# Scores of the second and third attention: one head to each half of TensorE's rows, two banks at a time, keys kept in one copy

## What is computed

```python
# second attention
q, k, v = (x @ qkv_w + qkv_b)          # 12 heads of 64
q = layernorm(q, q_norm_w, q_norm_b); k = layernorm(k, k_norm_w, k_norm_b)
attn = softmax(einsum('bhqd,bhkd->bhqk', q * 64 ** -0.5, k))
o = einsum('bhqk,bhkd->bhqd', attn, v) * gates
# third attention
q, k, v = x @ w_qkv.T                  # 12 heads of 64
q = q * rsqrt(norm(q, over heads) + eps); k = k * rsqrt(norm(k, over heads) + eps)
scores = softmax(einsum('bhid,bhjd->bhij', q, k) / scale)
out = einsum('bhij,bhjd->bhid', scores, v) @ w_out.T + b_out
```

## Time and profile before

| | us |
|---|---|
| median of 3 runs | 1297.73 |
| lowest and highest run | 1296.96, 1299.48 |
| the profiled execution | 1300.88 |
| its span, first to last instruction | 1299.1 |
| busy in the span: PE, PEld | 1191.0, 1042.0 |
| busy in the span: DVE, ACT, POOL | 953.1, 913.1, 437.0 |

### The profile page before, as it was taken

One profiled execution on the slowest core, in us unless ns is written; L12 is line 12 of the kernel. 1 busy time (PEld: TensorE's weight loads), 2 busy tenths in 40 slices (PEclk: granted clock), 3 DMA queues, 4 the chain that ended last, 5 costly groups with the idle time before them and its releaser, 6 DMA issues.

```text
span 1299.1 us, 25559 instructions
## 1 busy us (share of the span) xinstructions
PE 1191.0 (92%) x8302; PEld 1042.0 (80%) x8302; DVE 953.1 (73%) x2350; ACT 913.1 (70%) x3243; POOL 437.0 (34%) x477
## 2 busy tenths in 40 slices
PE   6998779895899999999869999999996898999998
PEld 3996557664788888889668998899884776999998
DVE  5668989875788888889547888888874888444434
ACT  1667788882798999899649889988985543444332
POOL 0001120302333333332034334433424401888755
PEclk9999999897899999999989999999998899999999
DMA  9302002000000000000030000000003342334100
GB/s 373 131 2 74 2 1 75 1 1 1 1 1 2 2 2 2 2 2 2 1 77 1 2 2 2 1 2 2 1 2 106 142 180 83 104 113 123 55 12 15
DMA packets 24590, 55.10 MB, mean 42 GB/s; under 512 B 3982, under 2 KB 21118, under 8 KB 23166
## 3 DMA queue, kind: packets, MB, share of 16 engines
q1 hardware_dynamic: 24460, 53.47, 12.4%
HBM read 39.31 MB, written 14.16 MB: 41 GB/s over the span
## 4 chain that ended last, share of the span: by engine, by line
PE 59%; DVE 9%; ACT 7%; issue 2%; POOL 1%; POOLq 0%; DVEq 0%; ACTq 0%
PE bank L1463 7%; PE bank L1428 6%; PE bank L1392 4%; DVE f_eq L1856 4%; PE bank L1454 4%; PE bank L1437 3%; PE bank L1412 3%; PE bank L1396 3%; PE bank L1393 3%; PE bank L1395 3%; PE bank L1394 3%; ACT t_p L1208 2%; PE bank L1965 2%; PE bank L1961 2%; PE bank L1966 2%; PE bank L1962 2%
## 5 line engine op out<-in xcount | busy, mean ns | idle before, releaser
L1208 ACT ACTIVATE t_p<-bank,t_nmax 108x108 f32<-108x108 f32 x792 | 267.2, 354 | 40.1 <-DVE t_nmax L737 39.3
L1044 POOL TENSOR_TENSOR t_sq<-t_raw 108x768 f32<-108x768 f32 x88 | 141.0, 1602 | 168.8 <-ACT t_raw L1148 168.4
L1428 PE MATMUL bank<-t_kS,t_qT 128*108 128x216 f32 (+1 forms) x660 | 179.1, 386 | 3.3 <-DVE h L328 2.5
L2090 POOL TENSOR_TENSOR f_hid_lo<-f_hid,f_hid_hi 128x432 fp32r<-128x432 f32 (+2 forms) x144 | 143.4, 1014 | 108.6 <-ACT f_hid_hi L2076 108.3
L1208 ACT ACTIVATION_READ_ACCUMULATOR t_p<-bank,t_nmax 108x1 f32 x792 | 166.0, 210 | 0.0
L755 DVE TENSOR_TENSOR t_p<-t_p,t_rinv 108x432 f32<-108x432 f32 x198 | 160.4, 810 | 6.8
L737 DVE TENSOR_REDUCE t_nmax<-bank 108x4 f32<-108x432 f32 x198 | 119.3, 603 | 59.3 <-PE bank L1428 59.0
L2076 ACT CAST f_hid_hi<-f_hid 128x432 fp32r<-128x432 f32 (+2 forms) x144 | 72.4, 515 | 117.7 <-DVE f_hid L2047 97.1
L1437 PEld LDWEIGHTS bank<-ident,t_p 108*108 108x108 f32 x792 | 86.6, 132 | 54.7 <-ACT t_pT L1216 35.0
L1437 PE MATMUL bank<-ident,t_p 108*108 108x108 f32 x792 | 107.4, 258 | 22.2 <-ACT t_pT L1216 21.0
L1428 PEld LDWEIGHTS bank<-t_kS,t_qT 128*108 128x108 f32 x660 | 110.6, 175 | 8.9 <-DVE h L328 2.5
(11 more groups left out here) (227 smaller groups left out, 3307.0 us busy)
## 6 DMA issues: line engine op xcount, KB each, us to landing
spilled<-f_slot SPq DMA_DIRECT2D x56, 216.0 KB, 1.9
f_slot<-spilled SPq DMA_DIRECT2D x56, 216.0 KB, 2.5
A_x<-in_x SPq DMA_DIRECT2D x5, 1728.0 KB, 18.5
A_w<-in_tok_w SPq DMA_DIRECT2D x5, 768.0 KB, 7.1
f_raw_down<-in_w_proj SPq DMA_DIRECT2D x1, 2304.0 KB, 11.0
out_tokens<-h SPq DMA_DIRECT2D x21, 81.0 KB
f_raw<-in_w_mfc SPq DMA_DIRECT2D x3, 512.0 KB, 4.6
f_raw<-in_w_mfc SPq DMA_DIRECT2D x6, 256.0 KB, 6.2
```

The lines of the kernel that those rows point to most:

```text
L1044: pool.tensor_tensor(sq, v, v, ALU.mult).then_inc(s["sq"], 1)
L1208: act.activation(b.p[g % 2][:, m, :], self.sbank[(3 * g + c) % 2][0:GT, n * GT:(n + 1) * GT], ACT.Exp, bias=b.nmax[:, m:m + 1], accum_out= ...
L1428: mm = pe.matmul(o[0:GT, n * GT:(n + per) * GT], b.qT[g % 2][:, hd // per, :], b.kS[g % 2][:, hd:hd + per, :], start=masked, stop=True, sk ...
L2090: pool.tensor_tensor(self.hid_lo[m % 4][:, c], self.hid[m % 4][:, c], self.hid_hi[m % 4][:, c].bitcast(F32), ALU.subtract).then_inc(s["lo" ...
```

## The change

- `scores` of C and D now comes twice in a turn. `scores(g, 0)` does eight heads: two mask matmuls over 432 columns, one into each score bank, and eight float32 matmuls of 64 rows and 108 columns, in which the head in the first 64 rows of a tile goes to one bank and the head in the other 64 rows to the other. `scores(g, 1)` does the last four heads in the same way, with masks of 216 columns. The middle one of the three places in TensorE's order is gone, and `scores(g, 1)` stands where `scores(g, 2)` stood.
- Both sides are kept once, in six tiles of 128 rows. `copy_qk` copies 128 rows in one instruction, in place of two of 64 rows, and the zeroing of `b.kS` is gone.
- The waits: `scores(g, c)` waits for `12 * g + 8 * c` exponentials, that is `scores(g, 0)` for all of the group before and `scores(g, 1)` for the first eight of its own group.
- The third row maximum comes in two instructions of two heads, since those four heads lie in two banks.
- The heads of a tile are put in another order (`ROWS`) in the prepared weights. B does what it did.

```diff
         def row_max(g, c):
-            after(dve, s["S"], nth(g, 3, c))
-            dve.tensor_reduce(b.nmax[:, 4 * c:4 * c + 4],
-                              self.sbank[(3 * g + c) % 2][0:GT, 0:4 * GT].rearrange("p (a n) -> p a n", n=GT),
-                              AX.X, ALU.max, negate=True).then_inc(s["max"], 1)
+            after(dve, s["S"], nth(g, self.s_parts, c if kind == "B" else c // 2))
+            bank = self.sbank[(3 * g + c if kind == "B" else c) % 2]
+            halves = [(bank, 4 * c, 4)] if kind == "B" or c < 2 else [(self.sbank[0], 8, 2), (self.sbank[1], 10, 2)]
+            for t, hd, n in halves:
+                dve.tensor_reduce(b.nmax[:, hd:hd + n], t[0:GT, 0:n * GT].rearrange("p (a n) -> p a n", n=GT),
+                                  AX.X, ALU.max, negate=True).then_inc(s["max"], 1)
...
-            for k in range(2):
-                dve.memset(b.kS[k][:, :, :], 0.0).then_inc(s["init"], 1)
...
         def copy_qk(g, u):
...
-                q = b.kS[g % 2][:, :, :].rearrange("p (t j) n -> p t j n", j=self.per_tile)
-                for j in range(self.per_tile):
-                    lo, hi = self.head_rows(j)
-                    if kind == "C":
-                        ins = act.activation(q[lo:hi, 3 * u:3 * u + 3, j, :], src[lo:hi, :, :], ACT.Identity,
-                                             scale=self.qk_affine[lo:hi, 0:1], bias=self.qk_affine[lo:hi, 1:2])
-                    else:
-                        ins = act.copy(q[lo:hi, 3 * u:3 * u + 3, j, :], src[lo:hi, :, :])
...
+            to, t0, n = (b.kS, 3 * u, 0) if u < self.qk_uses // 2 else (b.qT, 3 * (u - self.qk_uses // 2), 2)
+            to = to[g % 2][:, t0:t0 + 3, :]
+            if kind == "C":
+                act.activation(to, src, ACT.Identity, scale=self.qk_affine[:, n:n + 1],
+                               bias=self.qk_affine[:, n + 1:n + 2]).then_inc(s["Tev"], 1)
...
         def scores(g, c):
...
-            after(pe, s["exp"], nth(g, 12, 4 * c - 1) - 4)
...
+            after(pe, s["exp"], 12 * g + 8 * c)
+            tiles, heads = (4 * c, 4) if c == 0 else (4, 2)
+            for t in self.sbank:
+                pe.matmul(t[0:GT, 0:heads * GT], self.owner[:, :], self.other[:, 0:heads * GT], start=True, stop=True,
                           skip_group_check=True)
...
+            for n in range(heads):
+                for j in range(2):
+                    lo, hi = self.head_rows(j)
+                    mm = pe.matmul(self.sbank[j][0:GT, n * GT:(n + 1) * GT], b.qT[g % 2][lo:hi, tiles + n, :],
+                                   b.kS[g % 2][lo:hi, tiles + n, :], start=False, stop=True, skip_group_check=True)
             mm.then_inc(s["S"], 1)
...
-            if this:
-                scores(g, 1)
             if before:
                 turn_p(g - 1, 2)
...
             if this:
-                scores(g, 2)
+                scores(g, 1)
             if before:
                 values(g - 1, len(self.pv_split) - 1)
```

More of the change, by code:

```diff
@@ L628, in __init__ @@
         self.x_tiles = 3 if small else 2
-        self.inits = {"B": 7, "C": 13, "D": 1}[kind]
+        self.inits = {"B": 7, "C": 11, "D": 1}[kind]
+        self.s_parts = 3 if small else 2
+        self.max_parts = 3 if small else 4
     def turned(self, what, g, n=0):
@@ L672, in turn_bank, with scored, scores_of @@
         return banks[self.place(at) % len(banks)]
+    def scored(self, g):
+        return nth(g, self.s_parts, self.s_parts - 1)
+    def scores_of(self, g, hd):
+        if self.kind == "B":
+            return self.sbank[(3 * g + hd // 4) % 2][0:GT, hd % 4 * GT:(hd % 4 + 1) * GT]
+        n = hd % 4 if hd < 8 else hd % 2
+        return self.sbank[hd // 4 if hd < 8 else (hd - 8) // 2][0:GT, n * GT:(n + 1) * GT]
     def head_rows(self, hd):
@@ L760, in scale_q @@
             if u == 2:
-                after(dve, s["S"], nth(g - 2, 3, 2))
+                after(dve, s["S"], self.scored(g - 2))
             t0 = 3 * (u - 2)
@@ L885, in vector @@
                 dve.memset(b.pick[k][:, :], -1.0).then_inc(s["init"], 1)
-            dve.wait_ge(s["init"], 8)
+            dve.wait_ge(s["init"], 6)
             for k in range(2):
@@ L1415, in scores @@
         def scores(g, c):
-            o = self.sbank[(3 * g + c) % 2]
-            after(pe, s["exp"], nth(g, 12, 4 * c - 1) - 4)
             self.evacuated(pe, "qk", g, self.qk_uses - 1, and_earlier=True)
-            masked = kind == "B"
-            if not masked:
-                pe.matmul(o[0:GT, 0:4 * GT], self.owner[:, :], self.other[:, :], start=True, stop=True,
-                          skip_group_check=True)
-            per = self.per_tile
-            for n in range(0, 4, per):
-                hd = 4 * c + n
-                mm = pe.matmul(o[0:GT, n * GT:(n + per) * GT], b.qT[g % 2][:, hd // per, :],
-                               b.kS[g % 2][:, hd:hd + per, :], start=masked, stop=True, skip_group_check=True)
+            if kind == "B":
+                after(pe, s["exp"], nth(g, 12, 4 * c - 1) - 4)
+                pe.matmul(self.sbank[(3 * g + c) % 2][0:GT, 0:4 * GT], b.qT[g % 2][:, c, :],
+                          b.kS[g % 2][:, 4 * c:4 * c + 4, :], start=True, stop=True).then_inc(s["S"], 1)
+                return
+            after(pe, s["exp"], 12 * g + 8 * c)
+            tiles, heads = (4 * c, 4) if c == 0 else (4, 2)
+            for t in self.sbank:
+                pe.matmul(t[0:GT, 0:heads * GT], self.owner[:, :], self.other[:, 0:heads * GT], start=True, stop=True,
+                          skip_group_check=True)
+            for n in range(heads):
[3 more added lines that the diff above has]
+                                   b.kS[g % 2][lo:hi, tiles + n, :], start=False, stop=True, skip_group_check=True)
             mm.then_inc(s["S"], 1)
@@ L2175, in layouts, with by_rows @@
     KQV = [1, 0, 2]
+    ROWS = [0, 4, 1, 5, 2, 6, 3, 7, 8, 10, 9, 11]
+    def by_rows(w):
+        w = w.reshape(-1, 3, HEADS, 64)[:, KQV]
+        return np.concatenate([w[:, :2][:, :, ROWS], w[:, 2:]], 1).reshape(len(w), 2304)
     src = np.asarray(L0_attn_W_qkv).reshape(3, 4, 16, 3, 16)[:, :, :, KQV]
```

24 lines of the change are left out of this document (8 added, 16 removed).

## The result

The changed kernel takes 1317.67 us (median of 4 runs, 1314.65 to 1318.98), beside 1298.61 us for the kernel before in the same session (4 runs, 1296.96 to 1300.73): a ratio of 1.0133, 95% interval 1.0117 to 1.0148. That is 17 us slower by the ratio and 19 by the medians, where 10.7 were predicted; it lies inside the range of 1288 to 1330. The profiled execution took 1318.98 us with a span of 1317.2, beside 1300.88 and 1299.1 before, so 18.1 us of span have to be found.

What follows compares the result with a forecast made beforehand. TensorE alone was taken to set the turns of C and D. Turns +16.1 us (11.7 in D, 4.4 in C) and openings -5.4 gave +10.7 on the median 1297.7, so 1308.4 us, range 1288 to 1330.

Steps and rivals of the forecast that it cites:

- The new wait: TensorE before the last scores block, now needing exps(g, 1): waits 1.19 us a turn in D, 0.82 in C.
- D's turn, +0.62: Steady turns of D: -0.57 of TensorE work plus 1.19 of wait, over 18.8 turns 11.7 us.
- C's turn, +0.25: Steady turns of C: -0.57 of TensorE work plus 0.82 of wait, over 17.5 turns 4.4 us.
- A pair at 0.095: Float32 scores matmuls: two halves by rows run at once, 0.095 us a pair, 0.11 its upper end.
- The third rival: Scores halves do not run beside each other: 0.095 us more per pair, +52.1 in all, 1349.8 us; chance 0.10.
- Into and out of the halves, 0.15 and 0.18: TensorE around scores blocks: changing from whole array to parts costs 0.15 us, changing back 0.18.
- The first rival: Scores parts by rows cost no mode change: turn 0.48 us shorter, -6.7 in all, 1291.0 us; chance 0.12.
- TensorE's own work, -0.57 a turn: Scores blocks on TensorE: first +0.54, middle -0.91, last -0.20 us, together 0.57 less a turn.
- The whole copies, 0.51 and 0.31: ScalarE's whole copies replacing pairs of half copies: 0.51 us in C, 0.31 in D, saving 0.78 and 0.59.
- The openings, -5.4: Starts of C and D: two memsets gone, 2.6 us, and shorter opening copies of group 0, -2.8.
- The first and the last turns, 0: First and last turns, paced by ScalarE: shorter copies cancel longer first block and new wait, 0 with 4 us either side.
- the fourth rival: Wait before the last scores block about a third shorter, 0.3 us a turn, -11: 1297.8 us, no change; chance 0.08.

Runs made afterwards that it cites:

- experiment 1: Kernel before, only the third block of scores in C and D waiting for the first eight exponentials instead of four: 1339.04 us, ratio 1.0286.
- experiment 9: Changed kernel with ScalarE's norm_root(g+5) and roots(g+1, 1) moved ahead of gate_exp and copy_p(g-1, 1), copy_p(g-1, 2) behind exps(g, 1): 1269.27 us, ratio 0.9770.
- experiment 10: Kernel before with the same ScalarE moves as experiment 9: 1291.29 us, ratio 0.9932.

## Why the prediction came out right, and where it missed

- *The new wait decides.* Right, and shown from both sides: experiment 1 has it without the halves (+37 us), experiment 9 has the halves without it (-30 us, of which the moved work alone gives 9, by experiment 10).
- *D's turn, +0.62.* Measured +0.76. TensorE arrives at 881.06 + 0.28 = T0 + 6.46 (6.47 was said); the mask starts at T0 + 7.83 where the sum had 7.66, a wait of 1.37 for 1.19. Of this 0.17, 0.08 are in ScalarE's pieces and 0.09 in the release, which is 882.71 - 882.57 = 0.14 and not 0.05. Over 17 turns it gave 12.0 for 11.7, as the 18.8 turns of the estimate take in some of the opening.
- *C's turn, +0.25.* Measured +0.11, and the step that failed is the first one, that TensorE waits for nobody there. It reads 160.00 of 160 us busy, and still the kernel before loses 0.25 us a turn of C, which experiment 10 gets back by moving work on ScalarE alone (14.19 for 14.44). One such place in the kernel before:

```profile
519.12 0.44 PE L1412 MATMUL bank<-ident,t_raw 108*128 108x108 f32 x3
519.54 0.38 PE L1368 MATMUL bank<-ident,t_xf 108*128 108x108 f32 x2
```

  Three of these matmuls take 0.28 in the chain of waits; here the next starts 0.42 after them. A row's end is that of its last matmul, 0.44 behind its start, and covers the gap. In the changed kernel this pause is gone: from the last block's mask to the next T0 it is 518.60 - 511.39 = 7.21, where the prediction left 14.69 - 7.31 = 7.38. It is gone in experiment 1 too, where ScalarE's work is that of the kernel before, so it goes because TensorE waits elsewhere in the turn. With it the sum closes: -0.25 for the pause, -0.53 for TensorE's work and +0.88 for the wait (0.82 was said) are +0.10.
- *A pair at 0.095.* Right. The block of 16 takes 0.94 and that of 8 takes 883.57 - 883.00 = 0.57, so four pairs are 0.37, or 0.093 each. The third rival is out. The Trainium skill (TensorE: Matmul & The Clock Gate, the section on packing, The mechanism) lets weight loads of different row groups overlap; the trace agrees, at 108 columns.
- *Into and out of the halves, 0.15 and 0.18.* Right in the sum. The first float32 matmul starts 0.46 behind the start of the two masks (0.36 of work, 0.10 late), the second pair another 0.09 late; behind the block `turn_p` is 0.09 late and its second matmul 0.05. T0 to `turn_p` is 1.40 us, the sum had 1.45. The first rival, no cost at all, is out. The Trainium skill (TensorEngine Tiling (Array Packing), Key Properties) has a change of mode drain the array, and the trace agrees.
- *TensorE's own work, -0.57 a turn.* Measured -0.53 in C, by experiments 9 and 10; in D no pair of runs is free of other waits.
- *The whole copies, 0.51 and 0.31.* Measured 0.52 (L1201 starts at 508.17, the copy behind it at 508.69) and 0.32.
- *The openings, -5.4.* The first of C gave -3.4 for -4.2, at a clock that isn't the same in the two, so it can't be checked closer. That of D gave +1.8 for -1.2: the stretch to D's first output has the new wait in it twice, 1.37 and 1.21 us, which the estimate left out. Experiment 1, which has the wait alone, is 2.5 us longer there than the kernel before. The clock has a part in both, 0.88 in this stretch for 0.90 before.
- *The first and the last turns, 0.* This is the term that was mis-sized: the two ends gave +4.9 and +3.8, 8.7 us in all, over twice the 4 that I allowed. I had set shorter copies against a longer block. Two things are in it. 5.9 us are idle time of TensorE; the chain at the end of D shows how the values, the copy and the output of the group before follow the new wait one after another. 2.8 us are busy time that is longer at a lower granted clock, which the sum didn't have at all. The wait by itself gives most of the idle time: in experiment 1, which has it alone, TensorE is idle for 6.49 and 6.70 us in the two ends, 4.0 more than before. Those ends are only 1.6 and 1.2 us longer than before, at a clock of 0.96 and 1.00. Whether the added idle time brings the lower clock of the changed kernel, no run shows.
- *The feed-forward, 0.* It is 2.5 us shorter though nothing in it is changed. TensorE's 1568 instructions are busy there for 283.97 us in place of 286.80, at a clock of 0.97 for 0.96, which is enough for the difference; no run tests it otherwise.
- Two small sums on record are off and change nothing: 2 x 0.78 + 2 x 0.59 is 2.7 and not 2.8, and the fourth rival comes to 1297.5 and not 1297.8.

In sum: -4.2, +4.4, 0, -1.2, +11.7 and 0 were forecast for the first stretch, C's turns, the ends, D's opening, D's turns and the feed-forward, and -3.4, +1.4, +8.7, +1.8, +12.0 and -2.5 came. The direction and the mechanism hold. Of the 7.4 us that were missing, the ends are 8.7; the others nearly cancel (C's hidden pause, -3.0, against D's opening, +3.0), and that they do is luck.

## What to carry to other kernels

When a change lets an engine do its work in fewer, larger blocks, write down for each block which of the others' results it now needs one step earlier, and put that time against the arrival of the engine, turn by turn: here 0.5 us of work saved met a new wait of 0.9 us in C and 1.4 in D. If it loses there, look first for the idle time that the change itself opens on the other engine, and move into it work that nobody waits for. Of six reorderings of the changed kernel only the one that filled such a gap beat the kernel before. Three others got back a part of the loss, one none of it, and one cost 8%; each left a wait under another name. And price the filling and the draining of the pipeline apart from its steady turns, with the granted clock of each stretch beside it before you put a difference down to the change.

## What the runs showed of the hardware

- Float32 matmuls of 64 rows in different halves of the rows run beside each other with weights of 108 columns, 0.093 to 0.095 us a pair, the same as for the values, whose weights have 64 columns.
- They needn't be neighbours: with four instructions of one half ahead of four of the other all run in pairs (0.57 us, as alternating). With eight ahead of eight the block takes 1.41 us, between 0.94 (alternating) and the estimate of 1.7 for one at a time, and by the starts the second half begins beside the fifth instruction of the first.
- An engine shown as busy for 160.00 of 160 us can still lose 0.25 us a turn to another engine, because the ends of matmuls lie behind the start of the next.
- Between the steady parts of two stages the granted clock drops to its lower level for a while, and not at the same places in two kernels: the same twelve matmuls took 2.20 us at 1.00 and 3.71 at 0.58, and the last four intervals of C ran at 0.96 before and 0.86 after.
